# A graph layer in fp32: x turned by VectorE in 32x32 blocks into PSUM in every fourth group, the selection split in two, shifts moved ahead

## The reference, cut to what matters

```python
msg = relu(x[src] + edge_attr)                       # 25,000 edges, dst sorted
h   = x + segment_sum(msg, dst, num_segments=50000)  # 50,000 nodes, 128 features
h   = relu(relu(h @ W1 + b1) @ W2 + b2)              # 128 -> 256 -> 128
out = layernorm(x + h)                               # over the 128 features, eps 1e-5, fp32
```

## Time and profile before

| | before |
|---|---|
| median of 3 runs | 458.8 us |
| profiled execution, its own time | 458.92 us |
| its span | 457.5 us |
| TensorE clock granted, mean | 0.997 |
| busy: PE, PEld, DVE, ACT, POOL | 450.5, 379.9, 433.9, 394.8, 368.5 us |
| DMA moved | 86.82 MB in 83,870 packets, 190 GB/s |

### The profile page before, as it was taken

How to read it: one execution, slowest core, us unless ns; L and a number is a source line. 1 busy time by engine, 2 the same in 40 slices (tenths; PEclk the granted TensorE clock), 3 DMA queues, 4 the chain that set the end, 5 groups by cost and what they waited for, 6 DMA issues and landing times.

```text
span 457.5 us, 10683 instructions
## 1 busy us (share of the span) xinstructions
PE 450.5 (98%) x3050; PEld 379.9 (83%) x3050; DVE 433.9 (95%) x1760; ACT 394.8 (86%) x930; POOL 368.5 (81%) x402
## 2 busy tenths in 40 slices
PE   8999999999999999999999999999999999999995
PEld 7888888888888888888888888888888888888884
DVE  6899999999999999999999999999999999999997
ACT  3599888888888889988888888888888888888886
POOL 7777888888888878768888888888888888888842
PEclk9999999999999999999999999999999999999998
DMA  6576666666666666666666666666666666666642
GB/s 151 155 227 198 202 184 200 198 195 203 181 196 206 178 197 205 182 190 204 197 203 191 200 193 195 190 195 200 198 194 199 188 197 206 181 202 195 197 126 90
DMA packets 83870, 86.82 MB, mean 190 GB/s; under 512 B 12023, under 2 KB 79508, under 8 KB 83812
## 3 DMA queue, kind: packets, MB, share of 16 engines
q1 hardware_dynamic: 75044, 68.77, 48.5%
q0 software_dynamic: 8496, 17.38, 14.1%
q10 hardware_dynamic: 272, 0.00, 0.0%
HBM read 60.51 MB, written 25.60 MB: 188 GB/s over the span
## 4 chain that ended last, share of the span: by engine, by line
PE 96%; DMA 2%; DVE 1%; ACT 0%; issue 0%; DVEq 0%
PE h_ps L1061 38%; PE h1T_ps L1053 36%; PE hT_ps L977 11%; PE hT_ps L972 9%; DMA window<-in_pairs_dram,window_start_i 1%; DMA x_src<-in_x_dram,first_pairs 1%; DMA first_pairs<-in_pairs_dram 0%; PE hT_ps L948 0%; DVE stats L707 0%; PE hT_ps L965 0%; DVE z L700 0%; ACT std L863 0%; ACT h1T L858 0%; PE hT_ps L1001 0%; PE hT_ps L998 0%
## 5 line engine op out<-in xcount | busy, mean ns | idle before, releaser
L135 POOL DMA_INDIRECT x_src<-in_x_dram,src_of x254 | 269.4, 1061 | 66.8 <-issue 59.6
L1061 PE MATMUL h_ps<-w_sb,h1T 128*128 128x128 f32 x1564 | 197.5, 276 | 0.0
L1053 PE MATMUL h1T_ps<-hT,w_sb 128*128 128x384 f32 x520 | 188.5, 485 | 0.0
L1061 PEld LDWEIGHTS h_ps<-w_sb,h1T 128*128 128x128 f32 x1564 | 185.2, 192 | 0.0
L858 ACT ACTIVATE h1T<-h1T_ps,b_sb 128x384 f32<-128x384 f32 (+1 forms) x262 | 151.5, 580 | 36.9 <-PE h1T_ps L1053 28.5
L1053 PEld LDWEIGHTS h1T_ps<-hT,w_sb 128*128 128x128 f32 x520 | 88.7, 191 | 34.2
L877 ACT ACTIVATE y<-z,shift,rstd 128x128 f32<-128x128 f32 x263 | 114.6, 483 | 1.3 <-DVE shift L727 0.4
L607 POOL TENSOR_SCALAR y<-z,rstd,shift 128x128 f32<-128x128 f32 x123 | 87.1, 708 | 13.6 <-DVE shift L727 9.0
L977 PE MATMUL hT_ps<-sel,msg_hi 128*128 128x216 f32 x250 | 94.8, 447 | 0.0
L707 DVE BATCH_NORM_STATS2 stats<-z 128x6 f32<-128x128 f32 x391 | 88.7, 282 | 0.1
L972 PE MATMUL hT_ps<-ident,x_sb 128*128 128x128 f32 x375 | 87.5, 272 | 0.0
(11 more groups left out here) (139 smaller groups left out, 187.4 us busy)
## 6 DMA issues: line engine op xcount, KB each, us to landing
x_sb<-in_x_dram SPq DMA_DIRECT2D x130, 192.0 KB, 2.4
out_dram<-y SPq DMA_DIRECT2D x130, 192.0 KB
pre_msg<-in_edge_attr_dram SPq DMA_DIRECT2D x130, 128.0 KB, 2.8
x_src<-in_x_dram,src_of POOLq DMA_INDIRECT x254, 3.0
w_sb<-in_w_dram SPq DMA_DIRECT2D x2, 128.0 KB, 2.6
dst_rows<-in_dst_dram SPq DMA_DIRECT2D x1, 97.7 KB
x_src<-in_x_dram,first_pairs POOLq DMA_INDIRECT x6, 2.9
b_sb<-in_b_dram SPq DMA_DIRECT2D x1, 64.0 KB, 3.2
```

Source lines behind the costliest of these rows:

```text
L135: nc.gpsimd.indirect_dma_start(out=c["x_src"][:, g % EB, k, :], out_offset=None, in_=x, in_offset=bass.IndirectOffsetOnAxis(ap=index, axis ...
L1053: nc.tensor.matmul(h1T_ps[h][:, 0:n, 0:p], w1_sb[:, h * 128:(h + 1) * 128], hT[:, 0:n, 0:p], start=True, stop=True).then_inc(h1_summed, 1)
L1061: last = nc.tensor.matmul(h2_ps[g % 2][0:p, t, :], h1T[:, h, t, 0:p], w2_sb[:, h, :], start=(h == 0 and t == 0 and not biased(g, c)), stop ...
```

## The change

Four edits:

1. In the 29 groups 10, 14, ..., 122 (`BLOCK_GROUPS`) x is loaded a second time, by four DMAs of 32 partitions each (`start_blocks`), into `x_blocks`, so that 32 nodes lie on 32 partitions and a block of 32 features of each of four such sets follow one another. Each DMA gathers 384 runs of 32 values (128 bytes), 1,536 per group. VectorE turns every 32x32 block in one instruction of 384 values per partition and writes it into the bank `prep_ps1` (`turn_blocks`); TensorE then adds its four message matmuls onto it (`sum_onto_blocks`), with no x matmuls.
2. Group 9 forms its sum in `prep_ps1` too, by the old matmuls.
3. `select` is two comparisons of 216 values with a per-partition scalar, in place of one comparison of 432 values with a broadcast tensor.
4. In VectorE's round the `reciprocal` goes ahead of `low_part` and the `shifts` ahead of `add_x`.

```diff
+BLOCK = 32
+OPENING_GROUP = 9
+BLOCK_GROUPS = range(10, 126, 4)
+BLOCKS_AHEAD = 4
...
+def start_blocks(sp, x, g, c):
+    src = x[g * G:(g + 1) * G, :].rearrange("(a i t) (b j) -> b i t a j", i=BLOCK, t=T, j=BLOCK)
+    for b in range(128 // BLOCK):
+        sp.dma_start(c["x_blocks"][b * BLOCK:(b + 1) * BLOCK, :, :, :], src[b, :, :, :, :]).then_inc(c["blocks_loaded"], 16)
...
-    bank_of = {1: c["prep_ps"][1]}
+    bank_of = {1: c["prep_ps"][1], **{g: c["prep_ps"][1] for g in (OPENING_GROUP, *BLOCK_GROUPS)}}
...
             if inside(g - 4):
                 store(sp, g - 4)
+            if block_turned(g + BLOCKS_AHEAD):
+                if blocks_to(g + BLOCKS_AHEAD) > 1:
+                    sp.wait_ge(blocks_turned, blocks_to(g + BLOCKS_AHEAD) - 1)
+                start_blocks(sp, x, g + BLOCKS_AHEAD, c)
...
-                nc.vector.tensor_tensor(sel[:, g % EB, :, :], node_in_range[:, :, :].to_broadcast([128, K, T * WP]),
-                                        dst_of[:, g - FIRST_ROW:g - FIRST_ROW + 1, :].rearrange("p a k -> p k a").to_broadcast([128, K, T * WP]),
-                                        ALU.is_equal).then_inc(sel_ready, 1)
+                for k in range(K):
+                    last = nc.vector.tensor_scalar(sel[:, g % EB, k, :], node_in_range[:, 0, :], dst_of[:, g - FIRST_ROW, k:k + 1], None,
+                                                   ALU.is_equal)
+                last.then_inc(sel_ready, 1)
+
+        def turn_blocks(g):
+            dve.wait_ge(hT_copied, (OPENING_GROUP if blocks_to(g) == 1 else g - BLOCK_GROUPS.step) + 1)
+            dve.wait_ge(c["blocks_loaded"], 16 * (128 // BLOCK) * blocks_to(g))
+            nc.vector.transpose(c["prep_ps"][1][:, 0:T * 128], c["x_blocks"][:, :, :, :].rearrange("p t a j -> p (t a j)")).then_inc(blocks_turned, 1)
...
             add_bias(g)
+            if inside(g - 2) and g < END:
+                reciprocal(g - 2)
             if inside(g + 2):
                 low_part(g + 2)
-            add_x(g)
-            if inside(g - 2) and g < END:
-                reciprocal(g - 2)
-            statistics(g)
             if inside(g - 2) and g < END:
                 shifts(g - 2)
+            add_x(g)
+            statistics(g)
...
             if inside(g + 3):
                 add_edge_attr(g + 3)
+            if block_turned(g + 3):
+                turn_blocks(g + 3)
...
+        def sum_onto_blocks(g):
...
+            pe.wait_ge(blocks_turned, blocks_to(g))
+            pe.wait_ge(sel_ready, g - FIRST_GROUPS + 1)
+            pe.wait_ge(msg_hi_ready, parts_to(g, c) + 1)
+            add(0, msg_hi)
+            add(1, msg_hi)
+            pe.wait_ge(msg_lo_ready, parts_to(g, c) + 1)
+            add(0, msg_lo)
+            add(1, msg_lo, stop=True).then_inc(hT_summed, 1)
```

More of the change, by code:

```diff
@@ L124, in start_x, with block_turned, blocks_to @@
     sp.dma_start(c["x_sb"][0:partitions(g, c), slot, 0:tiles(g, c), :], rows(x, g, c)).then_inc(c["x_loaded"][slot], 16)
+def block_turned(g):
+    return g in BLOCK_GROUPS
+def blocks_to(g):
+    return sum(block_turned(i) for i in range(g + 1))
+def start_blocks(sp, x, g, c):
+    src = x[g * G:(g + 1) * G, :].rearrange("(a i t) (b j) -> b i t a j", i=BLOCK, t=T, j=BLOCK)
+    for b in range(128 // BLOCK):
+        sp.dma_start(c["x_blocks"][b * BLOCK:(b + 1) * BLOCK, :, :, :], src[b, :, :, :, :]).then_inc(c["blocks_loaded"], 16)
 def start_edge_attr(sp, edge_attr, g, first, c):
@@ L520, in main_path @@
     targets_ready = sem("targets_ready")
+    blocks_turned = sem("blocks_turned")
     sum_ready = sem("sum_ready")
@@ L699, in add_x @@
                 h2_of = h2[:, g % 2, :, :]
+            if block_turned(g):
+                dve.wait_ge(x_loaded[g % XB], (g // XB + 1) * 16)
             nc.vector.scalar_tensor_tensor(z[0:p, g % ZB, 0:n, :], h2_of[0:p, 0:n, :], 0.0, x_sb[0:p, g % XB, 0:n, :],
@@ L971, in turn @@
             def turn(t):
-                nc.tensor.matmul(hT_ps[:, t, :], x_sb[:, g % XB, t, :], ident[:, :], is_transpose=True,
+                nc.tensor.matmul(sum_bank(g)[:, t, :], x_sb[:, g % XB, t, :], ident[:, :], is_transpose=True,
                                  start=False, stop=False, skip_group_check=True)
@@ L976, in add @@
                 cols = sel[:, g % EB, k, :].rearrange("p (t q) -> p t q", t=T)
-                return nc.tensor.matmul(hT_ps[:, 0:T, LO[k]:LO[k] + WP], part[:, g % EB, k, :], cols,
+                return nc.tensor.matmul(sum_bank(g)[:, 0:T, LO[k]:LO[k] + WP], part[:, g % EB, k, :], cols,
                                         start=start, stop=stop, skip_group_check=True)
@@ L989, in sum_turned, with add @@
             turn(2)
+            add(1, msg_lo, stop=True).then_inc(hT_summed, 1)
+        def sum_onto_blocks(g):
+            def add(k, part, stop=False):
+                cols = sel[:, g % EB, k, :].rearrange("p (t q) -> p t q", t=T)
+                return nc.tensor.matmul(sum_bank(g)[:, 0:T, LO[k]:LO[k] + WP], part[:, g % EB, k, :], cols,
+                                        start=False, stop=stop, skip_group_check=True)
+            pe.wait_ge(blocks_turned, blocks_to(g))
[5 more added lines that the diff above has]
+            add(0, msg_lo)
             add(1, msg_lo, stop=True).then_inc(hT_summed, 1)
@@ L1094, in main_tensor @@
             hidden_sum(g)
-            if g + 1 < END:
+            if block_turned(g + 1):
+                sum_onto_blocks(g + 1)
+            elif g + 1 < END:
                 sum_turned(g + 1)
@@ L1412, in gnn_resnorm_kernel @@
             x_sb=sb("x_sb", [128, XB, T, D]),
+            x_blocks=sb("x_blocks", [128, T, 128 // BLOCK, BLOCK]),
+            blocks_loaded=sem("blocks_loaded"),
             ea_loaded=[sem(f"ea_loaded{u}") for u in range(EB)],
```

## The result

The changed kernel takes 454.5 us (median of 4 runs, 454.19 to 455.2) against 458.9 (4 runs, 458.74 to 458.96): ratio 0.9906, interval 0.9894 to 0.9918. It is faster by 4.35 us; the forecast was 7.8. The profiled execution took 454.33 us, 452.9 of it in the span.

What follows compares the result with a forecast made beforehand. TensorE was taken as the bound, before and narrowly after, with VectorE close behind. 458.9 - 9.0 (matmuls) + 1.2 (wait for `msg_lo`) = 451.1, median 451.0 us; range 449.0 to 461.0, the forecast's own 449.2 to 454 (chance 0.66).

Steps and rivals of the forecast that it cites:

- The matmuls removed: TensorE's sum in block groups: three turning matmuls dropped, 0.31 us saved in each of 29 groups, 9.0 us in all.
- VectorE the bound in all rounds: Rival: selects saving nothing and a turn of 0.6 make VectorE average 3.40 us a round; 461 us, chance 0.06.
- The reorder: VectorE's round: reciprocal ahead of `msg_lo` adds 0.11 us before it, leaving 0.20 in hand; shifts moved sooner cost nothing.
- The select pair: VectorE's select: two comparisons of 216 values take 0.40 us instead of 0.51, saving 0.11 in some 125 rounds.
- The turn: VectorE's new instruction in 29 rounds, 384 values from SBUF to PSUM: 0.48 us taken, between 0.33 and 0.96.
- The wait for `msg_lo`: TensorE at each block group waits 0.04 us because VectorE's bias is 0.24 late; 29 times, 1.2 us.
- The block loads: DMA queues: 128-byte packets at 27 ns, between 6.6 and 47, land before the turn; costed at nothing.
- POOL did not take the place: Rival judged: POOL cannot go below 3.38 us a round, gathers fall back; 455 us, within the 0.11 for partial loss.

Runs made afterwards that it cites:

- the shifts between and without the checks: Changed kernel with the shifts placed between z and the statistics, and without the input checks of VectorE's rounds 40 to 64: 449.99 us.
- the kernel with the shifts between: Changed kernel with only the shifts moved, to stand between add_x (which makes z) and the statistics: 451.70 us.
- the whole-row loads: Changed kernel with the four block DMAs reading runs of 1,536 bytes instead of 128, so h of the 29 groups is another: 454.54 us.
- the pair alone: Kernel before the change with only the select made into two comparisons of 216 values: 458.65 us.
- the two kernels with `pre_msg` sooner: Changed kernel with VectorE's old order and `pre_msg` ahead of the aggregation: 456.11 us; the same with the old select: 458.28 us.

## Why the direction was right and the size was not

**The matmuls removed: right.** With the shifts between and without the checks the kernel is 8.9 us faster than before, 0.31 for each of 29 groups, as summed.

**The step that failed** is this one: "On average VectorE needs 3.14 + 0.48/4 = 3.26 and TensorE 3.38 - 0.31/4 = 3.30: TensorE stays the bound, narrowly." In the changed kernel the distances between VectorE's biases, around one block group, are 3.09, 3.22, 3.28, 3.68, in all 13.27 us or 3.32 a round, and TensorE's four rounds are as long; without its wait they would be 13.22 (the kernel with the shifts between). What comes true of the rival "VectorE the bound in all rounds" is the outcome, by 0.05 in four rounds, and not its reasons (a select with nothing saved, a turn of 0.6) or its price of 461. The round without a turn was put at 3.14 and is 3.09 right behind a turn, where no wait for `msg_hi` is left, and 3.22 to 3.29 else. By terms:

- The reorder was priced by the reciprocal ahead of `msg_lo` only, and the shifts at nothing. What it took from behind z was missed: the statistics start 0.58 after z whatever stands between. The reciprocal gave nothing back there, so it adds its 0.08 to the round; the 0.16 from it to `msg_lo` in two rounds of four are these 0.08 and the rest of the wait for `msg_hi`, on which the prediction has no term. Moving the shift alone into that gap gave 2.8 us.
- The select pair costs 0.48 and not 0.40: 0.03 saved, inside the bounds (0.13 saved to 0.15 lost), but far from the value taken. Two scalar comparisons of 216 values do not lie on the line between 128 and 384. By the estimate from the Trainium skill, "VectorE: DVE Perf Modes", sections "The perf-mode tier table" and "The TRN2 errata", they would take 0.35; the measured 0.48 does not agree and is nearer to no gain, where the old select agrees with it (0.51 to 0.52).
- `pre_msg` was taken at 0.46 to the end of its record; with a ready instruction behind it, it takes 0.31. This error of 0.15 ran the other way and hid part of the two above: 3.14 + 0.12 + 0.08 + 0.05 - 0.15 = 3.24 (z to statistics, select, the reciprocal with the rest of the wait for `msg_hi` at 0.16 instead of 0.11, `pre_msg`). That the round was taken only 0.1 too short is luck in part, since these errors cancel.
- The turn: 0.50 against 0.48, no wait for its data. Right.

**The wait for `msg_lo`: the right number, by the path that was named.** The chain has 0.48 where 0.44 was summed, 0.04 as said. TensorE, ahead of the round with the turn and behind it:

```profile
306.92 1.46 PE L1106 MATMUL h1T_ps<-hT,w_sb 128*128 128x384 f32 x4
...
310.30 1.46 PE L1106 MATMUL h1T_ps<-hT,w_sb 128*128 128x384 f32 x4
```

The bias at 307.12 comes 0.20 after the first of these records, as in the kernel before (302.69 against 302.49): VectorE has caught up with TensorE and starts this round on time. The round lasts 3.67, so the next bias is 0.29 late and not 0.24, and TensorE waits 0.05, so its margin was some 0.24 and not 0.20: two errors of the same size, which is luck. With the shifts between the same round lasts 3.57, the bias is 0.19 late, and TensorE waits for nothing. The other account, that the four rounds together are too long (13.27 against 13.22), closes as well in this trace, since the bias at 307.12 would have gained nothing by coming sooner: `msg_lo` would still have waited for `msg_hi`. No run parts the two.

**A term was missing: the checks.** The sum spoke of steady rounds alone. Some 25 rounds carry extra VectorE work, which idle time and TensorE's margins hid before. With no slack left it costs 2.7 us, of the 3.5 by which the forecast was off. Of the 0.8 left, 0.6 are the block rounds at 3.13 where the sum has 3.38 - 0.31 + 0.04 = 3.11. The lost slack is not the whole reason for the 2.7: with the shifts between, where VectorE has 0.26 of idle in four rounds (the prediction's 3.30 and 3.26 leave 0.16), the checks still cost 451.7 - 450.0 = 1.7.

**The block loads: right that they cost nothing**, shown by the whole-row loads. A packet of 128 bytes took 12.9 ns, between the bounds of 6.6 and 47 and half of the 27 taken. SP was costlier than thought: the four issues take 2.65 us in the median, 2.95 in the burst below, and not 1.6.

```profile
303.99 2.95 SPq L145 DMA_DIRECT2D x_blocks<-in_x_dram  x4
```

They end at 306.9 and the turn stands at 310.29, 3.4 later, with no idle before it.

**POOL did not take the place** in the changed kernel: its gathers have 94.8 us of idle time before them (66.8 in the kernel before), 47.7 of it for ScalarE's copies.

```profile
L156 POOL DMA_INDIRECT x_src<-in_x_dram,src_of x254 | 265.4, 1045 | 94.8 <-ACT hT L889 47.7
L633 POOL TENSOR_SCALAR y<-z,rstd,shift 128x128 f32<-128x128 f32 x123 | 58.3, 474 | 12.6 <-DVE shift L762 7.8
```

Its tile of y took 474 ns, beside VectorE's statistics. Nor did the pair of comparisons block it by 0.4 us a round: with the pair alone the gathers went from 1061 to 1100 ns and the tile from 708 to 620. POOL does come into VectorE's way in the two kernels with `pre_msg` sooner, where nothing in the edit touches POOL.

**What could have been read in advance.** In the kernel before, VectorE has no idle in the round behind the first checks. Three rows of that trace:

```profile
157.40 0.55 DVE L681 TENSOR_TENSOR h<-h_ps,b_sb 128x384 f32<-128x384 f32 x1
158.02 0.42 DVE L672 SCALAR_TENSOR_TENSOR msg_lo<-pre_msg,msg_hi 128x256 fp32r<-128x256 f32 x1
...
160.74 0.55 DVE L681 TENSOR_TENSOR h<-h_ps,b_sb 128x384 f32<-128x384 f32 x1
```

The bias before the first stands at 154.22: a round at VectorE's own pace is 3.18 us, still without the wait for `msg_hi`. In the next, from 157.40 to 160.74, bias to `msg_lo` takes 0.62, 0.48 in a steady round. This is the wait that the old order meets as soon as VectorE is pressed, and with it the round is 3.34, only 0.04 below TensorE's 3.38 and not the 0.13 of the prediction's 3.25.

## What to carry to other kernels

When a change brings the second engine within a few hundredths of the first, read the second's round where it catches up (behind a stall), not where it idles: its steady gaps hide waits for results, its idle time hides extra work elsewhere in the run. An instruction that looks movable for nothing may be filling the time in which another waits for a result, so put a small independent one there. The same edit (a select of 0.48 instead of 0.51) was worth nothing before and 3.8 us after, so price an edit by the engine that will be the bound, in the kernel that will hold it.

## What the runs showed of the hardware

- VectorE started the statistics, which wait for z's 384 values, 0.58 to 0.59 us after z, and an independent instruction (the shift or the reciprocal) 0.47 after it.
- VectorE turned 384 values per partition in 32x32 blocks from SBUF to PSUM in 0.585 us in the mean of 29, 0.50 to the next start, and TensorE added onto what it wrote.
- An issue of a DMA with 384 runs of 128 bytes over 32 partitions took SP 0.61 us at the least, 0.625 in the median, with 32 runs of 1,536 bytes 0.41 and 0.42: the small runs took more of SP's time, and 12.9 ns a packet of the DMA engines, and neither cost the kernel any time.
- In the kernels with `pre_msg` sooner a shift of three values was held for 0.20 to 0.28 us when it began 0.40 to 0.49 into a gather on POOL, and for 0.09 when it began 0.22 to 0.26 into a tile of y. A tile of y on POOL took 0.95 us beside select and `pre_msg` and 0.45 beside the statistics. The Trainium skill, "SBUF — State Buffer", section "Who interferes with whom", says that a VectorE instruction with two SBUF inputs contends with a GpSimd instruction that reads SBUF, and that issue order decides who blocks. The lengths agree with that for the tile of y. The gather is another matter: in the changed kernel 35 shifts, behind `msg_lo` there and not behind the statistics, began 0.42 to 0.49 into a gather and none was held (0.07 to the next start), nor was `msg_lo` held 0.18 into one. So the overlap alone does not explain the hold, and no run tells what does.
